# A mixture-of-experts layer without its last stage: second-choice blocks add, normalise, take in the residual and write the output

## The reference

```python
# layer 0: f is an RWKV time mixing: k, v, r products, a log-space recurrence over time, an output product
# layer 1: f is a mixture of 8 experts with 2 chosen per token, plus one shared expert
logits = xf @ router_w
probs = softmax(logits); topw, topi = top_k(probs, 2)
ye = silu(xf @ w1[e]) @ w2[e]                       # for each chosen expert e
routed = sum over the two choices of topw * ye
shared = sigmoid(xf @ shared_gate_w) * (silu(gate) * up @ shared_down)
x = x + layernorm(routed + shared)
```

## Time and profile before

| what | value |
|---|---|
| median of 3 runs | 1736.05 us (1734.24 to 1737.11) |
| profiled execution, first to last instruction | 1778.9 us; no other time of it is given |
| TensorE busy | 1529.8 us (86%) |
| VectorE busy | 1410.4 us (79%) |
| ScalarE busy | 1315.6 us (74%) |
| GpSimd busy | 1110.4 us (62%) |
| bytes moved by DMA | 268.44 MB, mean 151 GB/s |
| granted TensorE clock, mean | 0.942 of full speed |

### The profile page before, as it was taken

The page is one execution under the profiler, slowest core; times in us unless marked ns, Lnnn a source line. Parts: engine busy times, 40 slices in busy tenths (PEclk is TensorE's granted clock), DMA queues, the critical chain, the costliest instruction groups (busy, mean ns, idle before and its releaser), DMA issues.

```text
span 1778.9 us, 35736 instructions
## 1 busy us (share of the span) xinstructions
PE 1529.8 (86%) x9960; PEld 1369.8 (77%) x9960; DVE 1410.4 (79%) x3406; ACT 1315.6 (74%) x2671; POOL 1110.4 (62%) x1063
## 2 busy tenths in 40 slices
PE   4899999999999999999999964799989999988200
PEld 3678888888888888888888853788888999988200
DVE  4798999999899898998989883677767776767256
ACT  3788889888888898988988873556656676666165
POOL 1245766767767677676776655255555588888655
PEclk8999999999999999999999986899999999999655
DMA  6122333333332332323332223788777688888999
GB/s 207 48 79 94 119 121 98 110 113 106 105 102 94 100 110 96 108 91 107 108 94 100 81 102 134 251 273 259 260 232 213 173 150 141 146 146 140 249 388 390
DMA packets 155152, 268.44 MB, mean 151 GB/s; under 512 B 19984, under 2 KB 94992, under 8 KB 154960
## 3 DMA queue, kind: packets, MB, share of 16 engines
q1 hardware_dynamic: 109264, 176.47, 30.7%
q0 software_dynamic: 45696, 89.70, 20.0%
HBM read 131.32 MB, written 134.77 MB: 150 GB/s over the span
## 4 chain that ended last, share of the span: by engine, by line
PE 57%; issue 9%; DVE 7%; DMA 7%; POOL 7%; ACT 3%; another core or an unknown queue 3%; DVEq 2%; SPq 1%; POOLq 0%; ACTq 0%
PE PS L1442 42%; PE PS L1622 5%; POOL d_y L631 4%; PE PS L1434 3%; PE PS L1638 3%; POOL d_xd L586 2%; DMA d_y<-xin,ixb 2%; PE PS L1505 2%; DMA d_y<-nx,ixb 1%; PE PS L1503 1%; DMA d_y<-x,ixb 1%; PE PS L1603 1%; DVEq L1405 1%; ACT sqo L939 1%
## 5 line engine op out<-in xcount | busy, mean ns | idle before, releaser
L586 POOL DMA_INDIRECT d_xd<-h2n,ixs x248 | 314.5, 1268 | 229.3 <-DVE h2n L1183 161.3
L1442 PE MATMUL PS<-hTh,wqh 128*128 128x512 f32 x768 | 306.5, 399 | 15.3 <-ACT kk L668 10.1
L1442 PE MATMUL PS<-hTl,wqh 128*128 128x512 f32 x768 | 305.9, 398 | 0.0
L1442 PE MATMUL PS<-hTh,wql 128*128 128x512 f32 x768 | 305.9, 398 | 0.0
L1442 PEld LDWEIGHTS PS<-hTh,wqh 128*128 128x128 f32 x768 | 146.4, 191 | 50.2 <-ACT kk L668 11.0
L1442 PEld LDWEIGHTS PS<-hTh,wql 128*128 128x128 f32 x768 | 146.0, 190 | 34.4
L1442 PEld LDWEIGHTS PS<-hTl,wqh 128*128 128x128 f32 x768 | 146.4, 191 | 33.3
L593 POOL DMA_INDIRECT d_xs<-ysh,ixs x124 | 133.0, 1072 | 47.0 <-issue 44.3
L1622 PE MATMUL PS<-hTh,shh 128*128 128x256 f32 x284 | 87.4, 308 | 25.7 <-DVE shl L1406 23.5
L1638 PE MATMUL PS<-weh,h2l 128*128 x380 | 106.7, 281 | 1.1 <-issue 1.0
L1638 PE MATMUL PS<-wel,h2h 128*128 x380 | 106.7, 281 | 0.5 <-issue 0.5
(11 more groups left out here) (306 smaller groups left out, 5767.6 us busy)
## 6 DMA issues: line engine op xcount, KB each, us to landing
xin<-in_L_attn_x SPq DMA_DIRECT2D x32, 512.0 KB, 4.2
x<-in_L_attn_x SPq DMA_DIRECT2D x32, 512.0 KB
d_x<-x SPq DMA_DIRECT2D x32, 512.0 KB
kk<-d_xd SPq DMA_DIRECT2D x36, 272.0 KB
vv<-d_xd SPq DMA_DIRECT2D x36, 272.0 KB
tr<-d_xd SPq DMA_DIRECT2D x35, 272.0 KB
dl<-d_xd SPq DMA_DIRECT2D x35, 272.0 KB
xin<-d_xs SPq DMA_DIRECT2D x24, 256.0 KB
```

What stands on the lines that cost most here:

```text
L586: g.indirect_dma_start(d_xd[s], bass.IndirectOffsetOnAxis(ap=ixs[:, m % 2, k:k + 1], axis=0), h2n_of(m)[:, j, :], None).then_inc(s_sct, 16)
L1442: ins = mm_(out_ap, l, r, start=(k == 0), stop=(k == len(todo) - 1))
```

## The change

The last stage is removed, and with it d_x1, d_y, its sinks, and the stores and loads of x1. A token's row now carries, beside its two weights, its position in the second-choice order, its token number, and two numbers from which the residual can be rebuilt: x1 = normed row times standard deviation plus mean (columns C_EXT and after, written by three new GpSimd instructions per chunk in `scale_h2` and `scatter`). First-choice blocks scatter their sum to d_ys at the second-choice position (`sums_out`). Second-choice blocks load that row as their starting value in place of the shared row (`load_result`), add weight times expert result, and then ScalarE sums the squares (`last_squares`), GpSimd makes the scale for two blocks at once (`last_scale`), VectorE rebuilds x1 (`back`) and adds the scaled result (`final`), and GpSimd scatters the row to the output (`tokens_out`). Padding rows carry a position out of bounds, and the scatters are given a bounds check that skips them. `ends` is gone, since weight and position now stand in fixed columns. Block rows and results both have 12 buffers; results are loaded five blocks behind block rows. A block's row buffer is free only when its scatter has landed. Before the first second-choice result is loaded, all first-choice scatters must have landed. Code of small instructions of the router, semaphores and waits that only follow from this is left out of the diff.

```diff
+    C_W, C_POS, C_TOK, C_EXT = D, D + 2, D + 3, D + 4
+    NEXT = XW - C_EXT
+    SKIP = 2.0
...
+    NX = NYB = 12
+    LY = 5
+    NPR = 4
+    NPAIR = (NB1 + 1) // 2
...
-    d_x1 = nc.dram_tensor("d_x1", [N, D], F32).ap()
-
-    x1_a = d_x1.rearrange("(c j p) d -> c p j d", j=NT, p=P)
-    x1_c = d_x1.rearrange("(c p j) d -> c p (j d)", j=NT, p=P)
-    out_c = out.rearrange("b (c p j) d -> (b c) p (j d)", j=NT, p=P)
+    out_r = out.rearrange("b t d -> (b t) d")
     d_xd = [nc.dram_tensor(f"d_xd{s}", [E * CAP + BLK, XW], F32).ap() for s in range(2)]
     d_xs = nc.dram_tensor("d_xs", [E * CAP + BLK, D], F32).ap()
 
-
-    NSINK = E + NB1 - NF + 1
-    d_y = nc.dram_tensor("d_y", [N + 1 + NSINK * BLK, D], F32).ap()
+    d_ys = nc.dram_tensor("d_ys", [E * CAP + BLK, D], F32).ap()
...
-        xb = [flat(t)[:, 0:2 * XW].rearrange("p (j d) -> p j d", j=2) for t in (kk, vv, tr, dl)]
+        old = [t[:, :, :, :, :].rearrange("p q s a n -> p (q s a n)").bitcast(F32) for t in (wqh, wql)]
+        old += [flat(t).bitcast(F32) for t in (wgh, wgl)]
+        xb = [old[i // 5][:, i % 5 * 2 * XW:(i % 5 + 1) * 2 * XW] for i in range(10)] + [t[:, 0:2 * XW] for t in old[2:4]]
+        xb = [t.rearrange("p (j d) -> p j d", j=2) for t in xb]
...
-        yb = [t[:, i:i + 2, :] for i in (0, 2) for t in (xin, nx, x1)]
...
+        yb = [flat(t)[:, i * 2 * D:(i + 1) * 2 * D].rearrange("p (j d) -> p j d", j=2)
+              for i in range(2) for t in (kk, vv, tr, dl, nx, x1)]
+        assert len(xb) == NX and len(yb) == NYB
+        xk = [flat(t)[:, i * 2 * D:(i + 1) * 2 * D].rearrange("p (j d) -> p j d", j=2) for t in (ysh, xin) for i in range(2)]
...
+        def landed(w):
+
+            return s_yo[w % NYB], 32 * (w // NYB + 1)
...
+                sp.dma_start(d_ys[E * CAP:E * CAP + BLK, :].rearrange("(p j) d -> p j d", p=P), zt[:, :, 0:D]
+                             ).then_inc(s_tail4, 16)
...
+                sp.dma_start(d_ys[bass.ds(r, BLK), :].rearrange("(p j) d -> p j d", p=P), zt[:, :, 0:D]).then_inc(s_tail4, 16)
...
-                if on(i - 4):
-                    sp.wait_ge(s_x1, n(i - 4, NT, NT))
-                    sp.dma_start(x1_a[i - 4], x1[:, :, :]).then_inc(s_st1, 16)
                 if 0 < i - 3 < NCH:
-                    sp.wait_ge(s_st1, 16 * (i - 3))
                     sp.wait_ge(s_h2, n(i - 3 - 1, NT, NT))
...
             def load_block(b):
-                if b >= 4:
-                    sp.wait_ge(s_Tx, b - 3)
-                    sp.wait_ge(s_tl, 2 * (b - 3))
+                if b >= NX:
+                    sp.wait_ge(*landed(b - NX))
                 s = b // NB1
                 r = sp.value_load(tabx[0:1, s, b % NB1:b % NB1 + 1], min_val=0, max_val=E * CAP)
-                first_row[b % 3] = r
-                sp.dma_start(xb[b % 4], d_xd[s][bass.ds(r, BLK), :].rearrange("(p j) d -> p j d", p=P)
-                             ).then_inc(s_xb[b % 4], 16)
-
-            def load_shared(b):
-                if b >= NYB:
-                    sp.wait_ge(s_yo[b % NYB], 32 * (b // NYB))
-                sp.dma_start(yb[b % NYB], d_xs[bass.ds(first_row[b % 3], BLK), :].rearrange("(p j) d -> p j d", p=P)
-                             ).then_inc(s_yl[b % NYB], 16)
-
...
-            for b in range(NB):
+                first_row[b % (LY + 1)] = r
+                sp.dma_start(xb[b % NX], d_xd[s][bass.ds(r, BLK), :].rearrange("(p j) d -> p j d", p=P)
+                             ).then_inc(s_xb[b % NX], 16)
+
+            def load_result(w):
+
+                if w >= NYB:
+                    sp.wait_ge(*landed(w - NYB))
+                rows_in = d_xs if w < NB1 else d_ys
+                sp.dma_start(yb[w % NYB], rows_in[bass.ds(first_row[w % (LY + 1)], BLK), :].rearrange("(p j) d -> p j d", p=P)
+                             ).then_inc(s_yl[w % NYB], 16)
+
+            for b in range(NB + LY):
                 if b == NB1:
-                    sp.wait_ge(s_tab, 9)
+                    sp.wait_ge(s_tab, 5)
                     sp.wait_ge(s_tail2, 16 * E)
-                load_block(b)
+                if b < NB:
+                    load_block(b)
                 if b == 1:
                     shared_tails(ends)
                 if 3 <= b < 3 + E:
                     tail_2(b - 3)
-                if b == 3 + E + 7:
-
-                    sp.wait_ge(s_tail2, 16 * E)
-                    sp.wait_ge(s_tab, 9)
-                if 0 <= b - 2 < NB1:
-                    if b == 2:
+                if b >= LY:
+                    if b == LY:
                         sp.wait_ge(s_scy, 16 * NT * NCH)
                         sp.wait_ge(s_tail3, 16 * (E + 1))
-                    load_shared(b - 2)
...
-            for c in range(NCH + AHEAD):
...
-                    sp.dma_start(yC[c % NY], y_v[c]).then_inc(s_yl[c % NY], 16)
...
-                    sp.dma_start(out_c[m], oC[m % NO]).then_inc(s_out[m % NO], 16)
...
+                    if b - LY == NB1:
+                        sp.wait_ge(s_tail4, 16 * (E + 1))
+                        for w in range(NB1 - NYB, NB1):
+                            sp.wait_ge(*landed(w))
+                    load_result(b - LY)
+
+            for w in range(NB - NYB, NB):
+                sp.wait_ge(*landed(w))
...
+                    pool.wait_ge(s_ex, n(c - 4, 2, 2))
...
+                if m >= 2:
+                    pool.wait_ge(s_exc, m - 1)
+                g.tensor_tensor(ext[:, m % 2, :, 0], var[:, 2, :], rstd[:, 2, :], ALU.mult).then_inc(s_ex, 1)
+                g.tensor_copy(ext[:, m % 2, :, 1], nmx[:, m % 4, :]).then_inc(s_ex, 1)
 
             def scatter(m, s):
-                pool.wait_ge(s_h2, n(m, NT, NT))
+                if s == 0:
+                    pool.wait_ge(s_h2, n(m, NT, NT))
+                    pool.wait_ge(s_ex, n(m, 2, 2))
+                    g.tensor_copy(h2n_of(m)[:, :, C_EXT:XW], ext[:, m % 2, :, :]).then_inc(s_exc, 1)
+                    pool.wait_ge(s_exc, m + 1)
...
-                    g.memset(zt[:, :, 0:D + E], 0.0).then_inc(s_zt, 1)
-                    g.tensor_copy(zt[:, :, D + E:XW], sinki[:, :, :]).then_inc(s_zt, 1)
+                    g.memset(zt, 0.0).then_inc(s_zt, 1)
+                    pool.wait_ge(s_zt, 1)
+                    g.memset(zt[:, :, C_POS:C_TOK + 1], SKIP).then_inc(s_zt, 1)
...
+            def rows_at(w, j, col):
+                return bass.IndirectOffsetOnAxis(ap=xb[w % NX][:, j, col:col + 1].bitcast(U32), axis=0)
+
+            def sums_out(w):
+
                 pool.wait_ge(s_y, 2 * (w + 1))
-                if w < NB1:
-                    for j in range(2):
-                        g.indirect_dma_start(d_y, bass.IndirectOffsetOnAxis(ap=ixb[:, w % 8, j:j + 1], axis=0),
-                                             yb[w % NYB][:, j, :], None).then_inc(s_yo[w % NYB], 16)
-                else:
-                    if w == NB1:
-
-                        for i in range(NYB):
-                            pool.wait_ge(s_yo[i], 32 * ((NB1 - i + NYB - 1) // NYB))
-                    for j in range(2):
-                        g.indirect_dma_start(d_y, bass.IndirectOffsetOnAxis(ap=ixb[:, w % 8, j:j + 1], axis=0),
-                                             yb[w % NYB][:, j, :], None, compute_op=ALU.add).then_inc(s_yo[w % NYB], 16)
-
-            for c in range(NCH):
-                w = 3 + c % 2
-                pool.wait_ge(s_sqo, n(NCH + c, NT, NT))
-                if c >= 2:
-                    pool.wait_ge(s_res, n(c - 2, NT, NT))
-                g.tensor_scalar(var[:, w, :], sq[:, c % 2, :], 1.0 / D, EPS, ALU.mult, ALU.add).then_inc(s_va[w], 1)
-                pool.wait_ge(s_va[w], c // 2 + 1)
-                g.tensor_tensor(rstd[:, w, :], var[:, w, :], mhalf[:, :], ALU.pow).then_inc(s_rs[w], 1)
+                for j in range(2):
+                    g.indirect_dma_start(d_ys, rows_at(w, j, C_POS), yb[w % NYB][:, j, :], None,
+                                         bounds_check=E * CAP - 1, oob_is_err=False).then_inc(s_yo[w % NYB], 16)
+
+            def last_scale(q):
+
+                many = min(2, NB1 - 2 * q)
+                at = slice(0, 2 * many)
+                pool.wait_ge(s_sqw, 2 * (2 * q + many))
+                if q >= NPR:
+                    pool.wait_ge(s_fin, 4 * (q - NPR + 1))
+                g.tensor_scalar(varw[:, q % NPR, at], sqw[:, q % NPR, at], 1.0 / D, EPS, ALU.mult, ALU.add).then_inc(s_vaw, 1)
+                pool.wait_ge(s_vaw, q + 1)
+                g.tensor_tensor(rsw[:, q % NPR, at], varw[:, q % NPR, at], mh4[:, at], ALU.pow).then_inc(s_rsw, 1)
+
+            def tokens_out(v):
+                w = NB1 + v
+                pool.wait_ge(s_fin, 2 * (v + 1))
+                for j in range(2):
+                    g.indirect_dma_start(out_r, rows_at(w, j, C_TOK), yb[w % NYB][:, j, :], None,
+                                         bounds_check=N - 1, oob_is_err=False).then_inc(s_yo[w % NYB], 16)
+
+            for w in range(NB1):
+                sums_out(w)
```

(76 more changed lines are left out.)

176 lines of the change are left out of this document (42 added, 134 removed).

## The result

The changed kernel takes 1679.55 us (median of 4 runs, 1677.5 to 1681.43); the kernel before, timed beside it, 1736.58 (4 runs, 1734.24 to 1737.12). The ratio is 0.9677 with a 95% interval of 0.9665 to 0.9689: 57 us faster. Forecast were 85 us and 1651 us. The sign and the range held; the size is a third short.

The account below looks back on a forecast made before the run. TensorE bounds the first stage, GpSimd the second-choice pace, transfers the last 119 us. Terms -104 + 21 - 14 + 4 + 6 = -87 gave a span of 1692, scaled by 0.976 to -85 and 1651 us; range 1607 to 1700.

Parts of the forecast that it names:

- The end, -104: After TensorE's last matmul: the 119 us go, near 15 us (12 to 20) take their place, -104 us.
- First-choice stage, -14: First-choice blocks: less work and deeper prefetch bring 3.80 us a block to 3.6, -14 us (-32 to nothing).
- Second-choice stage, +21: Second-choice blocks: 4.0 us each against 3.70 now, +21 us (-4 to +64).
- VectorE's floor: Second-choice stage: VectorE's own instructions, with `back` and `final` added and `ends` gone, need 3.65 us a block.
- the ring: Second-choice stage: waits from y_out(w-4) through last_scale, scatters and SP's loads to y_out(w), 3.74 to 3.97 us a block.
- the slow power: GpSimd's last_scale, second-choice stage: the power takes 2.02 us when VectorE works beside it, 1.11 without.
- Start +4: First result load stands behind more block loads and tails, delaying y_out(0): +4 us (0 to 10).
- junction +6: Between the block stages: load_result(71) waits for all first-choice scatters, +6 us (4 to 10).
- A: First-choice stage: prefetch held it, so it falls to TensorE's 3.35 us a block; 1634 us in all; chance 0.24.
- B: Second-choice stage: ring or GpSimd goes to 4.6 us a block, +64 in place of +21; 1693 us; chance 0.21.
- C: Both block stages: bounds-checked scatters cost more than plain ones, making the kernel slower than before; chance 0.04.
- D: Last stage: its work is only moved into the blocks, not saved; rejected by bytes, no chance given.

Follow-up runs that it names:

- p_before: The kernel before, unchanged, profiled a second time: time 1736.29 us, span 1734.2 us.
- e1: Changed kernel with the second row's `back` moved from VectorE to ScalarE: 1668.71 us, ratio to the kernel before 0.9612.
- after: The changed kernel itself, without follow-up edits: 1679.55 us, ratio to the kernel before 0.9677.
- e2: Changed kernel with second-choice load_result(b) issued right behind load_block(b), not behind load_block(b + 5): 1664.21 us, ratio to the kernel before 0.9585.
- e4: Changed kernel with the edits of e1 and e2 together: 1639.23 us, ratio to the kernel before 0.9449.
- e6: e4 with the second-choice tails (16 stores of zeros) moved from steps 3 to 10 to steps 20 to 27: 1632.75 us, ratio 0.9408.
- e3: Changed kernel with first-choice block loads held back to four ahead, as before: 1677.47 us, ratio to the kernel before 0.9662.
- e8: e6 with the last last_scale covering three blocks in place of a pair and a single one: 1634.61 us, ratio 0.9423.
- e7_end_wait: e6 with GpSimd itself waiting at its end until the last scatters have landed: 1631.75 us, ratio 0.9398.

## Why the prediction was right and where it was not

- **What bounds the kernel**: the 119 us at the end were read rightly, and they are what the change removes. TensorE's 981 us in the first stage hid all edits there.
- **The end, -104**: the term that was worth most, and 11 us too large. 6.3 of them lie behind the last scatter's start: 3.2 us for its landing, where its own 0.97, the closing drain's 8.25 and 0.25 of final semaphores follow. 7.5 are GpSimd's backlog, put at three blocks' scatters and seven in fact. The end before was 122 us (TensorE's last matmul ended at 1612.4 of 1734.2 us in p_before), not the 119 that the prediction counted from 1660 in the first profile; this gives 3 back.
- **First-choice stage, -14**: wrong, and the largest miss of the sum. The step that failed is the first one: 3.80 us from the earlier trace rows was the pace of one odd execution. The runs show 3.34 before with a floor of 3.27, and the change gave 1.4 us behind block 12. The table of times said it beforehand: the profiled span was 42.9 us above the median of the runs, and a factor of 0.976 spread this over all terms, where 31 us of it stood in this one stage and made a term that wasn't there. With "nothing" in that stage the sum would have been -73.
- **Second-choice stage, +21**: the mechanism was right in both halves and mis-sized. VectorE's floor is 3.76, for 3.65, by `back`; the ring with its bound of 3.97 gave 4.11 on average, for the 4.0 taken: +27.7 us. The ring's sum was sound: alone it gives about 3.90 (e1). In after both limits act, and 0.10 us a block are lengthened instructions, a term that the sum lacked. That two limits stood 0.3 us apart is what e1, e2 and e4 show: 11, 15 and 40 us.
- **GpSimd**: the 3.4 to 3.8 us a block that the prediction gave held at the lower end. The power took 1.06 us on average in the second-choice stage of after, not the 2.02 that stood in the earlier trace rows, so the slow power that was weighed isn't there. But VectorE and GpSimd do hold each other up, as the rows of e2_results_in_step show: 15 w1l at 0.57 us for 0.41, the `back` of 16 blocks at 0.85 for 0.72, 32 scatters at 1.9 for 0.97. The Trainium skill's page "SBUF — State Buffer", section "SBUF: two separate sides", which the prediction weighed, says that of a VectorE operation in a two-port mode and a GpSimd operation the one that starts first keeps the shared ports and the other blocks; these rows agree in kind, though no run here shows in which mode w1l and `back` run. The prediction priced it at up to 0.53 us a block, on GpSimd and by `back` alone. It shows in the scatters, which take 1.25 us on average in e2 and 1.09 in e4_both for 0.97, and on VectorE, where it is 0.07 us a block in e2. Halving VectorE's `back` (e1) left the number of long scatters about as it was, 28 for 25.
- **Start +4 and junction +6**: measured +5.4 and +7.0, by the waits named; e6 shows that the start's cost goes with the stores in front of the loads: without them blocks 0 to 12 take 43.6 us, less than the 46.6 before.
- **Rivals**: A falls by p_before and e3. B (4.6 us) was not reached: 4.11. C falls by the 1.27 us. D falls by the windows: 19 us at a DMA share of 0.06, and 214.42 MB moved in all, where it was 268.44.

## What to carry over

When the profiled span is longer than the median of the runs, profile again before a stage of it is priced: in the ordinary executions here the span is about 2 us shorter than the time, and the 44.7 us of the odd one sat in two places and not in a factor. When work moves from a stage of its own into a loop, sum each engine's round first and then follow the queue that loads the loop's inputs: a load that stands behind another's wait inherits that wait, and moving one line gave 15 us here. Where two limits stand close together, as here, lifting both is worth more than the two gains apart (11 and 15 us, but 40 for both).

## What was not expected of the hardware

- GpSimd's closing drain ended 8.25 us after its last scatter in after, e1 to e6 and e8, and took 8.25 us from its own start in e7_end_wait, behind a wait; with the scatters long past, in p_before, 3.7 us behind the last power. In the changed kernel, which ends on a scatter, the drain adds some 7 us to the end (8.25 less the 1.2 at which SP is past the landing); in the kernel before, which ends on SP's stores, it adds nothing.
- A scatter with a bounds check started 1.27 us after its neighbour, a plain one 1.26, an accumulating one 1.86.
- A 128x256 tensor_scalar with two scalar columns took 0.32 us where those of the earlier trace rows took 0.26.
- One profiled execution of the same program was 44.7 us (2.6%) longer than two others, nearly all of it within two stretches; the cause stays open.
- Of the 142 last scatters 25 took over 1.5 us in place of 0.97 in after, 28 in e1 (up to 1.8) and 32 in e2 (1.9), and none in the kernels with both edits. In e2 each of them ends 0.09 to 0.14 us behind a w1l of VectorE or in front of a w1l that takes 0.57 us for 0.41. Why the kernels with both edits have none wasn't followed up.
